# Both tiles' gate, up and down products placed in one unit of a fused attention and FP4 feed-forward kernel

## The reference

```python
xn = layernorm(x)
# attention, per batch and head
scores = (q @ k.T) * 8 ** -0.5 + slope[h] * (j - i)
ctx = softmax(scores) @ v
attn = ctx @ Wo + bo
# feed-forward, each operand quantized in blocks of 16 along the contraction
gate, up = Q(xn) @ Q(w_gate).T, Q(xn) @ Q(w_up).T       # 128 -> 352
ffn = Q(silu(gate) * up) @ Q(w_down).T                  # 352 -> 128
out = x + attn + ffn
```

## Time and profile before

| | us |
|---|---|
| median of 3 runs | 804.6 (804.46 to 805.57) |
| the profiled execution | 801.33 |
| its span | 799.5 |
| PE busy | 736.7 (92%) |
| VectorE busy | 711.9 (89%) |
| ScalarE busy | 661.4 (83%) |
| GpSimd busy | 427.0 (53%) |

### The profile page before, as it was taken

How to read it: one execution, slowest core, us unless ns; L and a number is a source line. 1 busy time by engine, 2 the same in 40 slices (tenths; PEclk the granted TensorE clock), 3 DMA queues, 4 the chain that set the end, 5 groups by cost and what they waited for, 6 DMA issues and landing times.

```text
span 799.5 us, 14573 instructions
## 1 busy us (share of the span) xinstructions
PE 736.7 (92%) x4951; PEld 218.3 (27%) x4951; DVE 711.9 (89%) x1304; ACT 661.4 (83%) x1366; POOL 427.0 (53%) x449
## 2 busy tenths in 40 slices
PE   6399998999899999999999999999899999999987
PEld 2012222222223222322222332322222322222223
DVE  8998899999899899999999899999898999999930
ACT  4107988888888988898889989898888898898896
POOL 5792157563545658581736656662627372634351
PEclk9657999999999999999999999999999999999999
DMA  6730002041101020060101001240100100000000
GB/s 183 219 73 2 2 3 81 2 134 27 41 1 41 2 81 2 23 151 15 42 1 42 3 33 50 93 93 2 41 2 22 34 3 1 15 2 2 2 2 27
DMA packets 33042, 31.90 MB, mean 40 GB/s; under 512 B 4456, under 2 KB 26856, under 8 KB 32968
## 3 DMA queue, kind: packets, MB, share of 16 engines
q1 hardware_dynamic: 32840, 30.86, 14.3%
q10 hardware_dynamic: 128, 0.10, 0.0%
HBM read 15.91 MB, written 15.04 MB: 39 GB/s over the span
## 4 chain that ended last, share of the span: by engine, by line
PE 63%; DVE 25%; ACT 5%; POOL 4%; issue 3%; DMA 0%; POOLq 0%; SPq 0%; ACTq 0%; DVEq 0%
PE pv L1258 23%; PE mx L1228 23%; DVE neg_half L1079 20%; ACT probs L863 3%; PE low L1281 3%; PE low L1275 2%; PE low L1307 2%; PE low L1296 2%; PE low L1208 2%; POOL zb L645 1%; PE low L1288 1%; PE low L1322 1%; POOL mb L644 1%; DVE am L1048 1%; PE low L1204 1%
## 5 line engine op out<-in xcount | busy, mean ns | idle before, releaser
L1079 DVE TENSOR_REDUCE neg_half<-mx 128x1 f32<-128x512 f32 x1024 | 641.4, 683 | 50.9 <-PE mx L1228 46.0
L863 ACT ACTIVATE probs<-low 128x512 f32<-128x512 f32 x1006 | 549.9, 616 | 61.8 <-PE low L1247 52.1
L1228 PE MATMUL mx<-k_op,q_op 51*128 51x512 bf16 x1024 | 325.8, 394 | 40.1 <-DVE neg_half L1079 28.3
L1247 PE MATMUL low<-q_op,k_op 53*128 53x512 bf16 x1006 | 305.6, 384 | 0.0
L1258 PE MATMUL pv<-probs,v_op 128*32 128x512 f32 x2048 | 273.6, 606 | 3.4 <-ACT pv_s L961 1.4
L1228 PEld LDWEIGHTS mx<-k_op,q_op 51*128 51x128 bf16 x1024 | 68.7, 94 | 333.0 <-DVE neg_half L1079 285.9
L749 POOL TENSOR_TENSOR ctx_s<-pv_s,pv_r 128x128 f32<-128x128 f32 x32 | 13.0, 406 | 127.2 <-DVE pv_r L1097 126.9
L644 POOL TENSOR_SCALAR mb<-mb 128x960 f32<-128x960 f32 (+2 forms) x17 | 58.7, 3455 | 36.7 <-DVE mb L1068 36.3
L1247 PEld LDWEIGHTS low<-q_op,k_op 53*128 53x128 bf16 x1006 | 66.0, 94 | 7.4 <-ACT probs L863 6.1
L1258 PEld LDWEIGHTS pv<-probs,v_op 128*32 128x32 f32 x2048 | 40.3, 108 | 88.6 <-ACT probs L863 41.2
L728 POOL TENSOR_TENSOR hid<-gate_s,up_s 128x352 f32<-128x352 f32 x32 | 29.9, 935 | 51.8 <-ACT up_s L890 51.1
(11 more groups left out here) (162 smaller groups left out, 658.7 us busy)
## 6 DMA issues: line engine op xcount, KB each, us to landing
q_op<-q_rows SPq DMA_DIRECT2D x30, 192.0 KB, 3.9
k_op<-k_rows SPq DMA_DIRECT2D x30, 192.0 KB, 4.8
q_rows<-qp SPq DMA_DIRECT2D x8, 384.0 KB, 2.6
k_rows<-kp SPq DMA_DIRECT2D x8, 384.0 KB, 3.2
x_s<-in_L_attn_inputs_dram SPq DMA_DIRECT2D x8, 256.0 KB, 3.8
q_rows<-qp SPq DMA_DIRECT2D x8, 256.0 KB, 3.0
k_rows<-kp SPq DMA_DIRECT2D x8, 256.0 KB, 3.1
out_dram<-o_s SPq DMA_DIRECT2D x7, 256.0 KB, 2.3
```

What stands on the lines that cost most here:

```text
L863: nc.scalar.activation(probs[U % 3][:, 2 * g + x, :], bank("exp", U, j), ACT.Exp).then_inc(st_free, 1)
L1079: nc.vector.tensor_reduce(neg_half[m % 2][:, i + kh:i + kh + 1], slot("max", pos, kh), AX.X, ALU.max, negate=True).then_inc(mx_free, 1)
L1228: nc.tensor.matmul(slot("max", pos, kh), q, k, start=True, stop=True).then_inc(mx_full, 1)
L1247: nc.tensor.matmul(bank("exp", U, j), k_op[quad][r, g, kt * P:(kt + 1) * P], q_op[quad][r, g, half * HALF:(half + 1) * HALF], start=True, ...
```

## The change

`FROM_XT` has one entry for both tiles: gates at 2, ups at 6, hT from 22 on, downs at 27. Both gate products of a pair get the same unit, likewise both ups and both downs: the first is put, the second is given its unit without asking whether it is free. The two hT keep a unit each, one behind the other. By the planner, of 256 units 112 then have no middle job, 96 have one and 48 have two. The ring of banks, GpSimd's and VectorE's lists follow the plan. As `up0` and `up1` are then one unit, the maxima of the second tile's hidden values are moved one unit down, to `up1 + 3`, where the block scales follow them at once.

By unit of a pair (those of the pair before in brackets):

| unit | before | after |
|---|---|---|
| 0 | xT | xT |
| 1 | (down 1) | |
| 2 | gate 0 | gates |
| 4 | gate 1 | |
| 6 | | ups |
| 7 | up 0 | (hT 0), x maxima |
| 8 | (hT 0), x maxima | (hT 1), hidden maxima 0 |
| 9 | up 1, hidden maxima 0 | hidden maxima 1, scales |
| 10 | | inverses |
| 11 | (hT 1), hidden maxima 1 | scale_to_grid |
| 12 | scales | (downs), powers |
| 13 | (down 0), inverses | add_power |
| 14 | scale_to_grid | |
| 15 | powers | take_power |

```diff
--- before.py
+++ after.py
@@ -112,8 +112,7 @@
 
 
 
-FROM_XT = {("gate", 0): 2, ("gate", 1): 4, ("up", 0): 7, ("up", 1): 9, ("hT", 0): 23, ("hT", 1): 26,
-           ("down", 0): 28, ("down", 1): 31}
+FROM_XT = {"gate": 2, "up": 6, "hT": 22, "down": 27}
 ROUNDED = 13
 
 
@@ -146,11 +145,15 @@
     for p in range(NP):
         start = FFN_FIRST + FFN_STEP * p
         U = put(start, "xT", p)
-        for kind, t in FROM_XT:
-            U = U + (ROUNDED if (kind, t) == ("hT", 0) else 1)
+        for kind in FROM_XT:
+            U = U + (ROUNDED if kind == "hT" else 1)
             if p + 1 < NP or kind in ("gate", "up"):
-                U = max(U, start + FROM_XT[kind, t])
-            U = put(U, kind, p, t)
+                U = max(U, start + FROM_XT[kind])
+            U = put(U, kind, p, 0)
+            if kind == "hT":
+                U = put(U + 1, kind, p, 1)
+            else:
+                at[kind, p, 1] = U
     for b in range(1, B):
         for g in (2 * b, 2 * b + 1):
             U = norm_unit(b) + 1 + 4 * (g % 2)
@@ -1158,7 +1161,7 @@
                             x_maxima(p + 1)
                         if (U, i) == (up0 + 2, 1):
                             hidden_maxima(p + 1, 0)
-                        if (U, i) == (up1 + 2, 1):
+                        if (U, i) == (up1 + 3, 1):
                             hidden_maxima(p + 1, 1)
                         if (U, i) == (up1 + 3, 1):
                             block_scales(p + 1)
```

## The result

The changed kernel takes 832.6 us (831.1 to 833.4) against 804.6: 1.036 times the time, 95% interval 1.034 to 1.039. It is slower, inside the range of 811 to 838, and 6.1 above the forecast of 826.5. The profiled executions lie 31.0 apart, 801.33 and 832.34 around spans of 799.5 and 830.5. That of before lies 3.3 under its median and that of after 0.2, so I account for 31.0, where the medians are 28.0 apart. On 801.3 the sum of the prediction was 21.9, which makes 823.2 (the 823.6 in it is a slip of addition), so 9.1 us are to be explained.

The account below looks back on a forecast made before the run. Prediction: PE and VectorE bound each unit in a loop, by the larger of two sums. +7.4 + 20.9 - 2.9 - 4.5 + 1 = +22 us, on the median 826.5; forecast range 817 to 834 (64%), with two rivals 811 to 838.

Parts of the forecast that it names:

- gates, ups, downs, hT, extras, absorption: Loop on PE and VectorE: merged gates and ups +7.4 us, downs with VectorE's extra work +20.9, absorption -2.9.
- extras: VectorE's maxima, scales, inverses and powers: units 9 to 11 pay them without a PE job; with downs 1.44 us per pair.
- absorption: Transposes and projections falling into VectorE-bound units fill some of the loss: a third of one `pvT` per pair, -2.9 us.
- turns late on GpSimd, in the loop: GpSimd's list: PE's waits for turns fall from 6.8 to about 2.5 us, worth -4 to -5; worst case 0.
- the units from 245 on: Kernel's end: copies of `down_s`, `ctxT_s` and `o_s` move before the last exponentials on ScalarE, +1 us, between 0 and 1.8.
- Each unit costs the larger of its two sums: PE and VectorE, every unit: about the larger of two sums, leftover not carried on; two-gate units 3.46 us, downs 3.62.
- costs a whole job: Rival on PE: each second product costs a whole job, +9 us on the forecast, 835 us; chance 13%.
- slack isn't lent: Denies the rival that short units lend slack to long ones between PE and VectorE, 791 us; chance 6%.
- only what is merged counts: Rival on VectorE: its extra work stays hidden, so only merged products, turns and end count, 812 us; chance 13%.
- GpSimd or VectorE stalls anew: Rival: VectorE waits for `hid_ok`, or turns become late by add_power's 3.4 us eight times, +27, 853 us; chance 4%.

Follow-up runs that it names:

- e6: Changed kernel with the turns' two small operations taken from GpSimd's list and put on VectorE right behind the maxima; 841.3 us, ratio 1.048.
- e5: Kernel before with the turns' two small operations taken from GpSimd's list and put on VectorE right behind the maxima; 811.3 us, ratio 1.013.
- e12: Changed kernel with some turns' small operations on GpSimd placed between the two long ones of add_power or swish; 825.6 us, ratio 1.026.
- e11: Kernel before with some turns' small operations on GpSimd placed between the two long ones of add_power or swish; 794.4 us, ratio 0.988.
- e8: e5 with, of the change, only both down products put in unit 13; 823.0 us, ratio 1.025.
- e7: e5 with, of the change, only both gate products put in one unit; 815.8 us, ratio 1.016.
- e10: Changed kernel with 40 unread products on PE ahead of the turn of unit 141; 828.4 us, ratio 1.031.

## Why the prediction was right, and where not

In three pairs of kernels whose traces compare (after and before, e6 and e5, e12 and e11) the change costs 26.4, 26.2 and 26.2 us from unit 0 to unit 245, wherever the turns' operations stand. The steps of the sum, on the profiled executions:

| step | predicted | measured |
|---|---|---|
| gates, ups, downs, hT, extras, absorption | +25.4 | +24.9 |
| turns late on GpSimd, in the loop | -4.5 | -1.4 |
| granted clock behind unit 141 | none | +2.9 |
| the units from 245 on | +1 | +4.7 |
| sum | +21.9 | +31.1 (31.0, with the 0.1 ahead of unit 0) |

The first row is worked out: 26.4, less 2.9 and plus 1.4. The other two pairs agree: 24.6 from e6 and e5 with their stretched operations taken off (10.4 and 8.8), 25.3 from e12 and e11 without what units 151 and 152 take more in e12 (0.9). And adding up, for each of the 15 units, the length it has in most pairs where no other job falls into it gives some 40.3 before and 42.1 after, +1.8 to +1.9 per pair (predicted +1.90).

**Each unit costs the larger of its two sums: right.** Two products take 3.45 and 3.61 (predicted 3.46 and 3.62), so the second adds its instructions and no entry and exit; "costs a whole job" is out. The unit behind stays at 2.49 (2.55 behind the ups, with its hT), so slack isn't lent, as e8 shows by taking a job away: that rival is out too. In after, units 8, 9, 10, 11 and 13 take, in most pairs where nothing else falls into them, 2.66, 2.75 to 2.85, 3.14, 2.77 and 2.72 (predicted 2.67, 2.83, 3.23, 2.84, 2.73); so the extras are not hidden, and "only what is merged counts" is out. e7 and e8 give the gates and the downs one by one, 4.1 and 7.2 in the loop where 3.7 and 9.9 were expected.

The absorption of 2.9 is right only in the sum, and its form, a third of a `pvT` per pair, isn't what the units show. A `pvT` makes its unit 0.59 longer in both kernels (3.08 for 2.49, 4.04 for 3.45). In after, two that stand in unit 9 are given back by unit 10 (2.56 for 3.14), two in unit 10 by half in unit 11 (2.49 for 2.77). And two v projections of after stand in unit 10, which takes 3.16 with them and 3.14 without; elsewhere one costs 0.63 to 0.67.

**The step that failed is the one on GpSimd.** It said "swish has 3 and 4 to itself; only a turn in unit 14 stands right behind add_power", and looked only at add_power, take_power, scale_back and swish. The turns of unit 14 (125 and 245) wait for 1.4 and 1.6 on PE, not far from the 2.5 in sum. But those of units 21 and 141 fall into unit 0 of their pairs, and wait for 1.2 and 2.9. The trace shows what else is in the list ahead of 141: the parts of a k projection (up to 476.0), a normalised output with a wait of 2.15 for VectorE's `pv_r`, two add_down, then add_power, then an output addition. Unit 21 has the same parts and the same normalised output. One backlog of 3 us was worth as much as all the small waits that went. Taken as what their units are too long, the late turns sum to 8.3 us before and to 8.7 after (6.9 of these in the loop); taken as PE's idle time right ahead of them, to 6.8 and 7.4, where I had 2.5 left over. I had put 0 as this step's worst case, and with the last turn and the clock it was passed. The rival "GpSimd or VectorE stalls anew" is right in kind, at this one place, with the price of add_power; it is far from eight times. And I gave a late turn the price of its wait alone, and behind unit 141 the granted clock was 0.50 for 6.8 us, another 2.9. e10 shows that this price is separate and due to idle PE; e12 shows that both go when the turn is in time, 5.9 us together for one turn.

**Luck.** The forecast misses the median by 6.1 and the profiled execution by 9.1. The 3.0 between the two come from the execution of before that I had read, 3.3 under its median, and not from anything that the prediction reasoned. The sum was 21.9 where 31.0 were measured on the same execution of before, and the errors of GpSimd's step, the clock and the end all point the same way.

**The end was mis-sized.** From unit 245 on after takes 39.1 us and before 34.4. Of the difference 1.4 are a turn late by 1.8 (unit 245); 1.2 are hT, downs and ctxT ahead of the last exponentials (units 249 to 254), which is the predicted +1; 1.0 is half clock in unit 248, behind the idle stretch of 247; and 1.1 come from unit 247 itself, where PE waits for the last maxima. These go to memory and back as operands. SyncE's issues in after, for the turns of units 237 and 245:

```profile
771.39 0.31 SPq L539 DMA_DIRECT2D m_rows<-max_t  x1
772.74 0.99 SPq L542 DMA_DIRECT2D q_op<-m_rows  x2
795.15 0.31 SPq L539 DMA_DIRECT2D m_rows<-max_t  x1
798.11 0.99 SPq L542 DMA_DIRECT2D q_op<-m_rows  x2
```

The same store takes 1.35 us until the load may go, and then 2.96. For the last one this is 1.4 in before, e5 and e10, and 3.0 to 3.5 in after and the other ten. e10 has the program of after but for 40 products, and the short time, and its unit 248 has no half clock either. So it differs between executions, and within one (as here), and I can't put it down to the change; why it has two values stays open. The clock behind it can fall as well, since PE has little else to do there. In e12 this is worse:

```profile
791.40:796.00 4.60, 3.87 (x16) 0.46 (x16) 0.00 (x0) 3.12 (x7) 0.00 (x0) 0.50 0.00 0
796.00:802.00 6.00, 5.93 (x29) 1.63 (x29) 0.00 (x0) 3.98 (x10) 0.00 (x0) 0.60 0.00 0
```

That is the larger part of how a distance of 26.2 in the loop becomes one of 31 between the medians of e12 and e11. Some 3 to 5 us of the measured loss are thus of the last units.

**The price of a move on VectorE** was right for the reductions and powers. One small operation was dearer: in unit 151 the block scale lasts 0.86 instead of 0.19, from 517.26 to 518.12, beside GpSimd's `qr<-qf,qp` from 516.92 to 518.07. That unit takes 3.81, and without it the first row of the table would be some 0.7 smaller.

## What to carry to other kernels

Where two engines hand slots to each other, price a move unit by unit as the larger of two sums: a job is free only up to the slack of its own unit, two jobs in one unit use one slack and leave the other empty, and extra work of one engine and long work of the other belong in the same unit. Before moving steps on an in-order engine, walk its whole list past every small operation that someone waits for: placing the turns' operations between two long ones gave 1.2%, while placing them two units early cost 2.5%. An idle stretch on TensorE like the ones of 2.9 and 3.75 us here has to be priced twice, for itself and for the half clock behind it.

## What was not expected of the hardware

**The clock.** After 2.9 us of idle PE within unit 141 the granted clock was 0.50 for the next unit, then 0.83 and 1.00, and it stayed at 1.00 where 40 small products filled most of that time. The Trainium skill (TensorE: Matmul & The Clock Gate, What's actually happening) says that the throttled state is the default and activity releases it; 0.50 is the 1.2 GHz level, and the traces agree. How long the engine was idle doesn't decide alone: the turns of before left it idle for up to 1.7 us with the clock at 1.00 behind them, and the same 1.6 us of idle time in unit 151 were followed by 1.00 in after and by 0.50 for 3.4 us in e12. What tells these apart isn't shown by any run here.

**VectorE behind GpSimd.** Small operations on VectorE whose operands are all in SBUF took up to 2.2 us instead of 0.175, to the end of the GpSimd operation beside them. The Trainium skill (SBUF — State Buffer, Who interferes with whom) says that casts, `tensor_scalar` and operations with two SBUF inputs can contend with GpSimd for a shared pair of ports, and that whoever issues first holds it for the whole instruction. The 30 stretched ones of e5 and e6 agree. But in e6 six such operations (in e5 two) ran in 0.175 while a long `tensor_scalar` was under way on GpSimd, as the cast at 490.63 beside L647 from 488.42 to 491.84, and one was stretched beside the same line (0.89 at 440.90). What tells these apart isn't shown by any run here.
